# Linear attention: the input transposed from the resident residual, in six loads, with one bias pass per pair and the transpositions one step ahead

## The reference, cut to what matters

```python
q = softplus(x @ Wq.T + bq)          # 16 heads of 8
k = softplus(x @ Wk.T + bk)
v = x @ Wv.T + bv
kv = cumsum(k[..., :, None] * v[..., None, :], axis=positions)
k1 = cumsum(k, axis=positions)
out = einsum('zsD,zsDe->zse', q, kv) / sum(q * k1)
x = layernorm(x + out @ Wo.T + bo)
```

## Time and profile before

| | us |
|---|---|
| median of 3 runs | 2205.88 |
| lowest, highest | 2205.70, 2206.94 |
| the profiled execution | 2202.96 |
| its span in the profile | 2201.2 |
| busy in the span: PE, POOL, ACT, DVE | 1994.3, 1322.8, 1258.4, 1551.4 |
| mean granted TensorE clock | 0.968 |

### The profile page before, as it was taken

One profiled execution on the slowest core, in us unless ns is written; L12 is line 12 of the kernel. 1 busy time (PEld: TensorE's weight loads), 2 busy tenths in 40 slices (PEclk: granted clock), 3 DMA queues, 4 the chain that ended last, 5 costly groups with the idle time before them and its releaser, 6 DMA issues. The chain is left out here.

```text
span 2201.2 us, 47735 instructions
## 1 busy us (share of the span) xinstructions
PE 1994.3 (91%) x16155; PEld 1718.1 (78%) x16155; DVE 1551.4 (70%) x3978; ACT 1258.4 (57%) x3814; POOL 1322.8 (60%) x1485
## 2 busy tenths in 40 slices
PE   6799968999999999999999999999999839999971
PEld 3455547999999999999999999999999827888761
DVE  3799965777777777777777777777777725555654
ACT  3455545666666666666666666666666514444553
POOL 4688856566666666666666666666666533444564
PEclk9899979999999999999999999999999969999995
DMA  3411110000000000000000000000000022223334
GB/s 97 114 34 30 34 31 6 8 14 19 15 17 14 19 15 17 15 18 15 17 15 18 15 18 15 19 15 17 15 18 16 14 61 74 72 71 91 105 107 128
DMA packets 112148, 80.00 MB, mean 36 GB/s; under 512 B 11518, under 2 KB 105288, under 8 KB 111784
## 3 DMA queue, kind: packets, MB, share of 16 engines
q1 hardware_dynamic: 92420, 50.52, 8.3%
q0 software_dynamic: 8640, 17.97, 2.4%
q10 hardware_dynamic: 10852, 8.46, 1.4%
HBM read 44.34 MB, written 32.57 MB: 35 GB/s over the span
## 5 line engine op out<-in xcount | busy, mean ns | idle before, releaser
L745 POOL TENSOR_TENSOR x_prob<-x_prob,x_inv 128x496 f32<-128x496 f32 x514 | 521.7, 1015 | 501.8 <-DVE x_inv L916 347.9
L830 ACT ACTIVATE x_prob<-x_ps_S,x_nmax 128x248 f32<-128x248 f32 x1028 | 473.6, 468 | 250.4 <-DVE x_nmax L910 250.4
L910 DVE TENSOR_REDUCE x_nmax<-x_ps_S 128x2 f32<-128x496 f32 x515 | 344.4, 669 | 119.7 <-PE x_ps_S L519 119.7
L856 ACT COPY x_probT<-x_ps_T 124x512 f32<-124x512 f32 x512 | 300.6, 587 | 185.4 <-PE x_ps_T L1200 185.3
L517 PE MATMUL x_ps_S<-x_kT_lo,x_G_hi 128*128 128x248 f32 x1030 | 329.4, 320 | 0.0
L1200 PE MATMUL x_ps_T<-ident,x_prob 128*124 128x128 f32 x2048 | 318.6, 278 | 9.4 <-POOL x_prob L745 9.4
L1200 PEld LDWEIGHTS x_ps_T<-ident,x_prob 128*124 128x124 f32 x2048 | 235.6, 140 | 72.5 <-POOL x_prob L745 29.0
L519 PE MATMUL x_ps_S<-x_kT_hi,x_G_hi 128*128 128x248 f32 x1030 | 286.1, 278 | 0.0
L518 PE MATMUL x_ps_S<-x_kT_hi,x_G_lo 128*128 128x248 f32 x1030 | 285.0, 277 | 0.0
L1492 POOL DMA_INDIRECT sorted_results<-e_y,e_x_rows x142 | 145.8, 1026 | 198.8 <-DVE e_y L1621 189.3
L1142 PE MATMUL x_ps_O<-x_probT,x_V 124*64 124x128 f32 x4096 | 251.9, 276 | 0.5 <-ACT x_probT L856 0.5
(11 more groups left out here) (239 smaller groups left out, 4548.3 us busy)
## 6 DMA issues: line engine op xcount, KB each, us to landing
e_x_rows<-sorted_rows SPq DMA_DIRECT2D x142, 66.0 KB
x_nk<-latents SPq DMA_DIRECT2D x34, 124.0 KB
lin_x_rows<-in_x SPq DMA_DIRECT2D x32, 128.0 KB, 2.3
latents<-lin_nlat SPq DMA_DIRECT2D x32, 128.0 KB, 1.8
turned_rows<-w_rows SPq DMA_DIRECT2D x32, 128.0 KB, 1.7
e_all_xT<-turned_rows SPq DMA_DIRECT2D x32, 128.0 KB, 2.2
e_back<-sorted_results SPq DMA_DIRECT2D x16, 256.0 KB, 3.4
out_dram<-e_result SPq DMA_DIRECT2D x16, 256.0 KB
```

The lines of the kernel that those rows point to most:

```text
L745: nc.gpsimd.tensor_tensor(prob[:, k], prob[:, k], inv[:, k].unsqueeze(2).broadcast_to([P, 2, K]), ALU.mult).then_inc(prob_ready, 1)
L830: nc.scalar.activation(prob[:, k, h, :], ps_S[:, n % BANKS, h * K:(h + 1) * K], ACT.Exp, bias=nmax[:, k, h:h + 1], accum_out=total[:, k, h ...
L856: nc.scalar.copy(probT[0:KT, s % (2 * GANG)], ps_T[0:KT, s % 2, :]).then_inc(probT_ready, 1)
L910: nc.vector.tensor_reduce(nmax[:, k, :], ps_S[:, n % BANKS, 0:2 * K].rearrange("p (h k) -> p h k", h=2), AX, ALU.max, negate=True).then_in ...
```

## The change

X is loaded on SP in six transfers of 1, 3, 4, 8, 8 and 8 pairs, ahead of the steps, and PE transposes straight from X; `x_rows` and its 32 loads are gone, and so are ACT's four loads. The transpositions of pair t + 1 are placed behind the output projection of step t (those of pair 0 ahead of the first step). The bias of q and k becomes a tile of 64 rows x 2 x 256, zero except in row 0 (rounded value) and row 32 (rounded rest), and one pass of 64 rows of ones against its 512 columns fills both halves of the PSUM bank; the projections accumulate onto it. POOL clears that tile at the start, and in each step its addition to X waits for the transpositions of that pair.

```diff
--- before.py
+++ after.py
@@ -183,17 +183,19 @@
     NE = E + 1
     QK = 2 * D
     PAIRS = B // 2
+    CHUNKS = (0, 1, 4, 8, 16, 24)
+    LOW = 32
+    ROWS = 64
     with ExitStack() as stack:
         room = Room(nc, stack, "lin")
         w_rows = room.sbuf("w_rows", [P, 4, D])
         w = room.sbuf("w", [P, 4 * D])
-        b_qk = room.sbuf("b_qk", [1, QK])
-        b_qk_part = [room.sbuf(f"b_qk_{n}", [1, QK], F32R) for n in ("hi", "lo")]
+        b_qk = room.sbuf("b_qk", [ROWS, 2, QK])
+        b_qk_parts = room.sbuf("b_qk_parts", [ROWS, 2, QK], F32R)
         b_v = room.sbuf("b_v", [D, 1])
         b_v_wide = room.sbuf("b_v_wide", [D, P])
-        ones = room.sbuf("ones", [1, P], F32R)
+        ones = room.sbuf("ones", [ROWS, P], F32R)
         b_o = room.sbuf("b_o", [P, D])
-        x_rows = room.sbuf("x_rows", [P, 2, 2, D])
         turned = room.sbuf("turned", [P, 4, S])
         pos = room.sbuf("pos", [P, 2, 2 * QK])
         v = room.sbuf("v", [P, 2, 2, D])
@@ -222,12 +224,11 @@
         ps_den = room.psum("ps_den", [P, 512])
 
         w_loaded, bqk_loaded, bvo_loaded = room.sem("w_loaded"), room.sem("bqk_loaded"), room.sem("bvo_loaded")
-        res_loaded = [room.sem(f"res_loaded{n}") for n in range(4)]
-        x_loaded = [room.sem(f"x_loaded{n}") for n in range(2)]
+        x_loaded = [room.sem(f"x_loaded{n}") for n in range(len(CHUNKS))]
         lat_stored = [room.sem(f"lat_stored{n}") for n in range(2)]
         wT_psum, wT_ready = room.sem("wT_psum"), room.sem("wT_ready")
         set_ready = room.sem("set_ready")
-        b_hi_ready, b_lo_ready = room.sem("b_hi_ready"), room.sem("b_lo_ready")
+        b_hi_ready, b_lo_ready, zero_ready = room.sem("b_hi_ready"), room.sem("b_lo_ready"), room.sem("zero_ready")
         xT_psum, xT_ready = room.sem("xT_psum"), room.sem("xT_ready")
         aT_psum, aT_ready = room.sem("aT_psum"), room.sem("aT_ready")
         qk_psum, vy_psum = room.sem("qk_psum"), room.sem("vy_psum")
@@ -243,8 +244,6 @@
         square_ready, scale_ready, shift_ready = (room.sem(n) for n in ("square_ready", "scale_ready", "shift_ready"))
         x1_ready, nlat_ready = room.sem("x1_ready"), room.sem("nlat_ready")
         block = stack.enter_context(nc.Block())
-        QUART = B // 4
-
         def here(s):
             return there(s, PAIRS)
 
@@ -254,8 +253,15 @@
 
         @block.sync
         def _(sp):
+            def load_chunk(n):
+                first, end = CHUNKS[n] * 2, (CHUNKS + (PAIRS,))[n + 1] * 2
+                sp.dma_start(X[:, first * D:end * D].rearrange("s (b d) -> s b d", d=D),
+                             x[first:end].rearrange("b s d -> s b d")).then_inc(x_loaded[n], 16)
+
             for n, weight in enumerate(weights):
                 sp.dma_start(w_rows[:, n, :], weight).then_inc(w_loaded, 16)
+            for n in range(len(CHUNKS)):
+                load_chunk(n)
 
             def step(t, par):
                 s5 = t - 5
@@ -263,9 +269,6 @@
 
                     sp.wait_ge(nlat_ready, s5 * 2 + 2)
                     sp.dma_start(rows_of(lat, s5, slice(0, S)), nlat[:, 1 - par]).then_inc(lat_stored[1 - par], 16)
-                if here(t):
-                    wait(sp, xT_psum, t - 1)
-                    sp.dma_start(x_rows[:, par], rows_of(x, t, slice(0, S))).then_inc(x_loaded[par], 16)
                 if isinstance(t, int) and t == 5:
                     later.load(sp)
 
@@ -275,12 +278,11 @@
 
         @block.gpsimd
         def _(pool):
+            nc.gpsimd.memset(b_qk[:], 0.0).then_inc(zero_ready, 1)
             nc.gpsimd.memset(half[:], -0.5).then_inc(set_ready, 1)
             nc.gpsimd.memset(ones[:].bitcast(F32), 1.0).then_inc(set_ready, 1)
             pool.wait_ge(set_ready, 2)
             pool.wait_ge(bias_ready, 1)
-            for n in range(4):
-                pool.wait_ge(res_loaded[n], 16)
 
             def step(t, par):
                 s1, s2, s4 = t - 1, t - 2, t - 4
@@ -291,6 +293,7 @@
                                             ).then_inc(scale_ready, 1)
                 if here(s1):
 
+                    pool.wait_ge(xT_psum, s1 + 1)
                     pair = X[:, bass.ds(s1 * 2 * D, 2 * D)]
                     nc.gpsimd.tensor_tensor(pair.rearrange("p (b d) -> p b d", b=2), pair.rearrange("p (b d) -> p b d", b=2),
                                             b_o[:].unsqueeze(1).broadcast_to([P, 2, D]), ALU.add).then_inc(bias_added, 1)
@@ -314,14 +317,14 @@
 
         @block.scalar
         def _(act):
-            for n in range(2):
-                act.dma_start(b_qk[:, n * D:(n + 1) * D], biases[n].rearrange("(o d) -> o d", o=1)
-                              ).then_inc(bqk_loaded, 16)
+            act.wait_ge(zero_ready, 1)
+            for row in (0, LOW):
+                for n in range(2):
+                    act.dma_start(b_qk[row:row + 1, :, n * D:(n + 1) * D],
+                                  biases[n].rearrange("(o u d) -> o u d", o=1, u=1).broadcast_to([1, 2, D])
+                                  ).then_inc(bqk_loaded, 16)
             act.dma_start(b_v[:], biases[2].rearrange("(d o) -> d o", o=1)).then_inc(bvo_loaded, 16)
             act.dma_start(b_o[:], biases[3].rearrange("(o d) -> o d", o=1).broadcast_to([P, D])).then_inc(bvo_loaded, 16)
-            for n in range(4):
-                act.dma_start(X[:, n * QUART * D:(n + 1) * QUART * D].rearrange("s (b d) -> s b d", d=D),
-                              x[n * QUART:(n + 1) * QUART].rearrange("b s d -> s b d")).then_inc(res_loaded[n], 16)
             nc.scalar.preload_act_table_set("natural_log_exp_and_others")
             act.wait_ge(wT_psum, 1)
             nc.scalar.copy(w[:], ps_t[:]).then_inc(wT_ready, 1)
@@ -368,10 +371,11 @@
 
         @block.vector
         def _(dve):
-            dve.wait_ge(bqk_loaded, 32)
-            nc.vector.tensor_copy(b_qk_part[0][:], b_qk[:]).then_inc(b_hi_ready, 1)
+            dve.wait_ge(bqk_loaded, 64)
+            nc.vector.tensor_copy(b_qk_parts[:], b_qk[:]).then_inc(b_hi_ready, 1)
             dve.wait_ge(b_hi_ready, 1)
-            nc.vector.tensor_tensor(b_qk_part[1][:], b_qk[:], b_qk_part[0][:].bitcast(F32), ALU.subtract
+            low = slice(LOW, LOW + 1)
+            nc.vector.tensor_tensor(b_qk_parts[low], b_qk[low], b_qk_parts[low].bitcast(F32), ALU.subtract
                                     ).then_inc(b_lo_ready, 1)
             dve.wait_ge(bvo_loaded, 32)
             nc.vector.tensor_copy(b_v_wide[:], b_v[:].broadcast_to([D, P])).then_inc(wide_ready, 1)
@@ -453,21 +457,27 @@
             nc.tensor.matmul(ps_den[:, 0:D], b_v_wide[:], w[:, 3 * D:4 * D], start=True, stop=True).then_inc(bias_psum, 1)
             pe.wait_ge(set_ready, 2)
 
+            def turn_rows(t):
+
+                wait(pe, aT_ready, t - 3)
+                if t in CHUNKS:
+                    pe.wait_ge(x_loaded[CHUNKS.index(t)], 16)
+                for u in range(2):
+                    last = nc.tensor.transpose(ps_t[:, u * S:(u + 1) * S], X[:, (t * 2 + u) * D:(t * 2 + u + 1) * D],
+                                               ident[:])
+                last.then_inc(xT_psum, 1)
+
+            turn_rows(0)
+
             def step(t, par):
                 s1, s3 = t - 1, t - 3
                 if here(t):
-                    wait(pe, aT_ready, s3)
-                    pe.wait_ge(x_loaded[par], landed(t, par))
-                    for u in range(2):
-                        last = nc.tensor.transpose(ps_t[:, u * S:(u + 1) * S], x_rows[:, par, u, :], ident[:])
-                    last.then_inc(xT_psum, 1)
                     pe.wait_ge(xT_ready, t + 1)
                     wait(pe, pos_ready, t)
+                    nc.tensor.matmul(ps_qk[:], ones[:], b_qk_parts[:].rearrange("p u f -> p (u f)"), start=True, stop=False)
                     for u in range(2):
-                        out = ps_qk[:, u * QK:(u + 1) * QK]
-                        nc.tensor.matmul(out, ones[:], b_qk_part[1][:], start=True, stop=False)
-                        nc.tensor.matmul(out, ones[:], b_qk_part[0][:], start=False, stop=False)
-                        last = nc.tensor.matmul(out, turned[:, u, :], w[:, 0:QK], start=False, stop=True)
+                        last = nc.tensor.matmul(ps_qk[:, u * QK:(u + 1) * QK], turned[:, u, :], w[:, 0:QK], start=False,
+                                                stop=(u == 1))
                     last.then_inc(qk_psum, 1)
                 if here(s3):
                     pe.wait_ge(att_ready, s3 + 1)
@@ -491,6 +501,8 @@
                                                 start=True, stop=True)
                 if here(t) or here(s3):
                     last.then_inc(vy_psum, 1)
+                if here(t + 1):
+                    turn_rows(t + 1)
                 if here(s1):
 
                     pe.wait_ge(qk_ready, s1 + 1)
```

## The result

| us | before | after |
|---|---|---|
| median, measured side by side | 2205.79 (2205.43 to 2206.94, 4 runs) | 2178.97 (2177.95 to 2181.31, 4 runs) |
| the profiled execution, its span | 2202.96, 2201.2 | 2181.31, 2179.6 |
| mean granted TensorE clock | 0.968 | 0.969 |

The ratio is 0.9879 [0.9862, 0.9896]: 26.8 us faster, where 42 were forecast. In another session beside other runs of before, the same kernel gave 2177.09 and 0.9878 [0.9862, 0.9893].

A forecast was written before the change was run, and what follows sets the result against it. PE was taken to set linear attention's 8.13 us step, DVE close behind. Steps and weights 33.6 plus start 8.5 took 42.1 off 2202.96, giving 2160.9; with 2.9 between profile and median, 2164 us, range 2157 to 2181.

The forecast's parts named there:

- the likeliest case: Whole kernel: all gains occur as summed, 2164 us, own range 2158 to 2174, chance 0.66.
- Bound moves from PE to DVE (part 3): Linear attention step: PE would need only 6.77 us, under DVE's 7.36, so DVE takes over.
- The step, 7.36 (part 3): Linear attention: each step falls from 8.13 to 7.36 us, DVE's time in the last full step before.
- POOL's added wait on the transpositions: POOL in each linear attention step: met a whole step before, costing 0 to 0.05 us.
- The bound of 7.50 for the step: Linear attention: upper end for DVE's step, the steady 8.13 us less its 0.63 hole.
- another loop sets the step, 7.75, 2175: Rival: ACT's att chain or POOL sets linear attention's step at about 7.75, 11.3 us more, 2175; chance 0.18.
- Bias pass (part 2): PE, q and k projection: passes fall from 1.92 to 1.19 us (bounds 1.1 to 1.45), gaining 0.73 per step.
- Weights (part 4): Later weights' loading: PE's input no longer queues behind them; with the steps, net 33.6 us off.
- The new wait of 1.5 at the latents' store: ACT's normalisation of the fourth pair waits for the second store behind the weights: 0 to 3.5 us, taken 1.5.
- Start (part 6): Kernel start: earlier copy of weights and fewer bias passes, less slower first sums, gain 4.3 to 9.5 us, taken 8.5.
- output bias lands maybe 1 to 2 us later: Kernel start: the output bias transfer is delayed 1 to 2 us because the loads now run beside it.
- The clock rival: PE's waits in each step drop its clock from 2.4 to 1.2 GHz; 2344 if all steps slow; chance 0.04.

The follow-up runs named there:

- e5: Changed kernel with the output bias added by a PE bias pass instead of POOL's addition, v and output biases loaded first: 2165.31 us, ratio 0.9814.
- e1: Changed kernel with POOL's addition to X moved behind its two products of k and v: 2167.61 us, ratio 0.9835.
- e2: Changed kernel with two bias passes of 256 columns per sequence put back: 2181.45 us, ratio 0.9902.
- e3: Changed kernel with the transpositions of each pair put back to the head of their own step: 2176.87 us, ratio 0.9880.
- e7: Kernel before, with only the later weights issued two per step from step 5 instead of all at once: 2194.61 us, ratio 0.9949.
- e10: Changed kernel with output bias on PE, v and output biases loaded first, all X loads but the first held until all biases landed: 2160.98 us, ratio 0.9800.
- e9: Changed kernel with the five larger loads of X held until the v and output biases have landed: 2175.60 us, ratio 0.9864.
- c_after_again: The changed kernel itself, unaltered, measured once more in another session: 2177.09 us, ratio 0.9878.
- e6: Changed kernel with output bias on PE, v and output biases loaded first, and transpositions back at the head of their step: 2174.18 us, ratio 0.9874.
- e8: Kernel before, with only POOL's addition to X moved behind its two products of k and v: 2204.83 us, ratio 0.9999.

## Why the prediction was right in its direction and short in its size

The stated range of 2157 to 2181 held the time, and the likeliest case did not occur in full: the forecast was 42.1 off the profiled execution, the landmark shows 25.05. The 2179 measured lies outside the 2158 to 2174 that this case allowed for itself, and inside the range only by the room left for rivals, of which none occurred. That the range held is luck. By its own parts:

1. **Bound moves from PE to DVE (part 3):** right. DVE is never idle in the steady steps, PE waits 0.92 in front of the output projection, as announced.
2. **The step, 7.36 (part 3): the step that failed.** It measured 7.87, and 29 x 0.51 = 14.8 us is nearly all that is missing. The failed piece is twofold. I took DVE's bound from the tail, where L386 to L386 has no idle time; but that first product had come 0.64 late, behind PE, and its late start had kept POOL's addition (290.06) clear of L398 (290.76). The row was a bound for DVE alone, not for DVE beside a POOL that is level with it. And I priced "POOL's added wait on the transpositions" at 0 to 0.05, asking only whether POOL comes late; nothing in the sum asked which instruction of DVE it would now run beside. e5 reaches 7.35, so the sum of DVE's own work was right. The bound of 7.50 for the step fell for the same reason.
3. **The rivals:** "another loop sets the step, 7.75, 2175" has nearly the right time with the wrong cause: neither ACT's copies nor POOL's load set 7.87 (e1, e2 and e3 exclude both), but instructions that became longer by meeting. No rival had this mechanism.
4. **Bias pass (part 2):** mis-sized within its bounds. L477 to the transpositions of att took 154.75 - 153.36 = 1.39, forecast 1.19, upper bound 1.45. The pass takes 153.79 - 153.36 = 0.43 start to start, not the 0.23 of the earlier trace rows. It lies under DVE's bound and cost nothing.
5. **Weights (part 4):** the hole is gone, as said; e7 prices it at 11 to 13. The new wait of 1.5 at the latents' store did not come: the store went out at 60.85, 15.6 after the first weight instead of 17.5, and ACT asks for it three steps after its first normalisation, which at 7.87 is 23.6 us and not 22.1. The wait itself was a sound thought: in e10, whose steps are 7.34, ACT stands still for 2.86 us until that store has landed (2.27 and 2.48 in the steps beside it, waiting for DVE), and one step is 7.65. It is a matter of 0.3 us; e5, at nearly the same step, has none.
6. **Start (part 6):** forecast 8.5, measured 7.2 by the second product. The copy at 8.27 was right; "output bias lands maybe 1 to 2 us later" was the short term, and e9 shows the 3.8 us (2.4 to 3.8 over the profiles) that the loads of X add to it. Part of this came back, as the first running sums took 3.60 (4.46 in c_after_again) where up to 6.9 were feared. The low end of the start, 4.3, had left out the 1.4 for the dropped passes; with it, it is 5.7.
7. **Tail:** not in the sum, -1.75 here. In the repeated profile of the same kernel the last step took 7.86 (263.39 to 271.25) and its sums 3.60, so the same kernel runs with the loss and without. But it is no rarity: in ten of the fourteen profiles the last sums took 4.5 to 5.3 us, e7 among them, and in four (before, c_after_again, e6, e8) 3.60. What decides it was not tested.
8. **The clock rival:** granted 1.00 from 100 to 150 us, although PE waits in each step. It did not occur there; the 0.89 from 260 to 270 us, with PE busy 6.84 of the 10, is that of point 7, and in c_after_again the same window has 1.00 with the same 6.84.

With the measured terms: 42.1 - 14.8 - 1.3 + 1.5 - 1.75 = 25.8, the landmark's 25.05 within 0.8.

## What to carry to other kernels

When a bound moves from one engine to another, the idle time that goes had a second effect: it kept instructions of DVE and POOL apart in time. Before you forecast a step by adding up one engine's durations, shift the rows of the other by the idle time that will vanish, and look which of them then overlap, above all those with two operands in SBUF (e1's L441 met POOL's quotient with a single one). And where an addition can be folded into a matmul that has spare time, it takes the meeting away along with the work.

## What the hardware showed that I had not expected

Two instructions on different engines, with no semaphore between them, make each other wait whole instructions. Where POOL's addition starts 0.02 us after DVE's L402 (0.68), it takes 1.24 instead of 0.73, and the next instruction of DVE, on 4 elements a row, takes 0.68 instead of 0.15 and ends with it; where the addition starts first, at 184.74, it is L402 that takes 1.13. DVE's product, with one input in PSUM, kept its 1.21 beside POOL's products, and the reduction its 2.55. The Trainium skill has this rule (SBUF — State Buffer, section Who interferes with whom): a DVE instruction with two inputs in SBUF and a GpSimd instruction that reads SBUF take the same read port by an exclusive lock, and the one that comes second is blocked for the whole of the other. The traces agree in each row named here, the unlengthened ones too. One row asks for more than this sentence: L441 of e1 has one tensor input and constants, and was lengthened all the same, while the reciprocal beside POOL's moved addition (159.39), also with one input, kept its 0.34. Before the forecast I had held that rule against no row.

A transfer of 64 KB took 5.6 to 7.0 us to land beside the loads of X (258 GB/s in all from 6.4 to 13.4 us of after), and 3.2 when those were held back (e9, 23 GB/s from 6.4 to 9.6). The 512-column pass with 64 rows took 0.43 start to start, nearly twice the 0.23 of the earlier trace rows; no run here tells whether the rows, the fp32 passes behind it or the place in the stream makes the difference. At the very start such a pass ran for 0.79 against 0.50 later.
